# Half a chunk's second weight pass as pairs of 64-row matmuls, and a first normalisation shared by two engines

## What is computed

```python
xn = layernorm(x)                         # no scale, no shift, eps 1e-5
a  = silu(xn @ wA_gate.T)                 # 2048 x 2752
a[the half of each row that is smallest in |a|] = 0
s  = (a * (xn @ wA_up.T)) @ wA_down.T     # 2048 x 1024
g  = silu((silu(xn @ wB_gate.T) * (xn @ wB_up.T)) @ wB_down.T)
out = x + s * g
```

## Time and profile before

| what | us |
|---|---|
| median of three runs | 2845.15 |
| lowest and highest run | 2844.10, 2845.57 |
| the profiled execution, device time | 2844.23 |
| the same, span of the trace | 2842.5 |

### The profile page before, as it was taken

The page is one execution under the profiler, slowest core; times in us unless marked ns, Lnnn a source line. Parts: engine busy times, 40 slices in busy tenths (PEclk is TensorE's granted clock), DMA queues, the critical chain, the costliest instruction groups (busy, mean ns, idle before and its releaser), DMA issues.

```text
span 2842.5 us, 31407 instructions
## 1 busy us (share of the span) xinstructions
PE 2822.9 (99%) x12544; PEld 2349.2 (83%) x12544; DVE 1882.1 (66%) x2486; ACT 1209.3 (43%) x1202; POOL 661.6 (23%) x282
## 2 busy tenths in 40 slices
PE   7999999999999999999999999999999999999999
PEld 6888888888888888888888888888888888888887
DVE  3135989989312598998731168999872217899971
ACT  3335988223222477721122257771112225776110
POOL 5665443024644100000054410000005440000001
PEclk9999999999999999999999999999999999999999
DMA  6767888578432455556532245555653225555564
GB/s 223 244 237 279 291 288 287 200 258 321 161 97 98 160 194 194 194 195 240 200 133 96 94 175 193 194 194 192 245 185 132 96 92 189 192 192 193 192 226 173
DMA packets 100032, 549.95 MB, mean 193 GB/s; under 512 B 10992, under 2 KB 10992, under 8 KB 53104
## 3 DMA queue, kind: packets, MB, share of 16 engines
q1 hardware_dynamic: 99952, 548.97, 54.7%
HBM read 449.31 MB, written 99.61 MB: 193 GB/s over the span
## 4 chain that ended last, share of the span: by engine, by line
PE 99%; DVE 0%; POOL 0%; DMA 0%; issue 0%; DVEq 0%; SPq 0%; POOLq 0%
PE ps L383 33%; PE ps L481 11%; PE ps L482 11%; PE ps L483 11%; PE ps L456 11%; PE ps L459 11%; PE ps L457 11%; POOL hid_buf L729 0%; PE ps L438 0%; DVE stats L749 0%; DMA prods<-x 0%; POOL w_split L702 0%; DVE hid_buf L1027 0%; DVE prods L782 0%; DVE hid_buf L1025 0%
## 5 line engine op out<-in xcount | busy, mean ns | idle before, releaser
L702 POOL TENSOR_TENSOR w_split<-w_raw,w_split 128x1024 fp32r<-128x1024 f32 (+1 forms) x242 | 578.2, 2392 | 1700.1 <-ACT w_split L529 1522.3
L383 PE MATMUL ps<-w_split,hid_ring 128*128 128x512 f32 x4160 | 943.6, 389 | 0.0
L383 PEld LDWEIGHTS ps<-w_split,hid_ring 128*128 128x128 f32 x4160 | 781.0, 188 | 162.0
L815 DVE TENSOR_SCALAR_CACHE_REDUCE ranks<-key_buf,cand 128x2752 int16<-128x2752 f32 x248 | 763.0, 3076 | 5.8
L549 ACT ACTIVATE signs_row<-key_buf,cand 128x2752 bf16<-128x2752 f32 x248 | 642.4, 2590 | 191.0 <-DVE cand L824 181.3
L456 PE MATMUL ps<-w_split,xnT 128*128 128x512 f32 (+1 forms) x1408 | 541.4, 384 | 0.4 <-POOL w_split L702 0.4
L848 DVE TENSOR_TENSOR prods<-ps,key_buf 128x512 f32<-128x512 f32 (+1 forms) x96 | 61.1, 636 | 725.2 <-ACT key_buf L567 725.2
L457 PE MATMUL ps<-w_split,xnT 128*128 128x512 f32 (+1 forms) x1408 | 540.8, 384 | 0.0
L483 PE MATMUL ps<-xnT,w_split 128*128 128x512 f32 x1376 | 535.3, 389 | 0.0
L482 PE MATMUL ps<-xnT,w_split 128*128 128x512 f32 x1376 | 535.3, 389 | 0.0
L481 PE MATMUL ps<-xnT,w_split 128*128 128x512 f32 x1376 | 535.3, 389 | 0.0
(11 more groups left out here) (75 smaller groups left out, 1320.0 us busy)
## 6 DMA issues: line engine op xcount, KB each, us to landing
w_split<-split SPq DMA_DIRECT2D x280, 1024.0 KB, 4.8
w_raw<-w_a SPq DMA_DIRECT2D x160, 512.0 KB, 3.4
split<-w_split SPq DMA_DIRECT2D x64, 1024.0 KB, 6.4
split<-w_stage SPq DMA_DIRECT2D x22, 1024.0 KB, 6.3
w_raw<-w_b SPq DMA_DIRECT2D x42, 512.0 KB, 4.5
w_stage_raw<-wd_b SPq DMA_DIRECT2D x22, 512.0 KB, 4.6
w_raw<-wd_a SPq DMA_DIRECT2D x22, 512.0 KB, 4.7
prods<-x SPq DMA_DIRECT2D x16, 512.0 KB, 5.8
```

Of the source, the lines that this page charges most:

```text
L383: ins = pe.matmul(ps[:, 2 * t + half, :], h, w[:, half * TB:(half + 1) * TB], start=(first and n == 0), stop=(last and n == 1))
L702: pool.tensor_tensor(w_lo[q][:, 0:w], w_raw[q][:, 0:w], w_hi[q][:, 0:w].bitcast(F32), ALU.subtract).then_inc(lo_ready, 1)
L815: dve.tensor_scalar(ranks[:, :], keys[:, t, :], cand_f[:, t:t + 1], 0.0, ALU.is_lt, ALU.add, accum_out=counts[:, t:t + 1]).then_inc(sel_st ...
```

## The change

**Down projections.** In the last chunk of each, `down_tile` makes one pass (high plane, weights' high part). The pass with the weights' low part becomes `down_rows`, ahead of it, for all four tiles: for each tile two matmuls of 64 rows. One uses rows 0 to 63 for the first 512 output columns, the other rows 64 to 127 for the second 512. The second needs the hidden values' high part on rows 64 to 127, and ScalarE writes it there, into the low plane (a new instruction of 64x512 in `hid_split`). In `down_last` the waits for all three chunks and `down_rows` stand ahead of the loop over tiles.

**Start.** ScalarE normalises tiles 0 and 1 (ACT_NORM = 2) in one instruction each, as x times `rstd` plus `shift`; VectorE makes `shift` and normalises tiles 2 and 3. TensorE issues 84 transposes of the identity into the last bank (WARM) ahead of the real ones, and takes the real ones by tile, in the order 2, 3, 0, 1, for the first four banks and then for the other four. VectorE, no longer POOL, makes the low part of weight tile 0; ScalarE's high part of tile 2 moves behind its eight copies.

```diff
--- before.py
+++ after.py
@@ -72,6 +72,9 @@
 OUT_POOL = 3
 
 
+ACT_NORM = 2
+WARM = 84
+
 K_ORDER = (4, 5, 6, 7, 0, 1, 2, 3)
 
 STATS_AT = 6
@@ -201,6 +204,7 @@
         var = small("var", [NT])
         rstd = small("rstd", [NT])
         newton = small("newton", [NT])
+        shift = small("shift", [NT])
         found = small("found", [NT], U32)
         bit = small("bit", [NT], U32)
         cand = small("cand", [NT], U32)
@@ -230,6 +234,8 @@
         xres_landed = [sem(f"xres_landed{t}") for t in range(NT)]
         ln_step = sem("ln_step")
         xn_normed = sem("xn_normed")
+        xn_shift = sem("xn_shift")
+        xn_scaled = sem("xn_scaled")
         xn_turned = sem("xn_turned")
         xn_squares = sem("xn_squares")
         xn_hi = sem("xn_hi")
@@ -377,12 +383,20 @@
                     hi = hid_ring[:, s, 0, t * P:(t + 1) * P]
                     lo = hid_ring[:, s, 1, t * P:(t + 1) * P]
 
-                    passes = ((hi, w_hi[q]), (hi, w_lo[q])) if last else ((hi, w_hi[q]), (hi, w_lo[q]), (lo, w_hi[q]))
+                    passes = ((hi, w_hi[q]),) if last else ((hi, w_hi[q]), (hi, w_lo[q]), (lo, w_hi[q]))
                     for n, (h, w) in enumerate(passes):
                         for half in halves:
                             ins = pe.matmul(ps[:, 2 * t + half, :], h, w[:, half * TB:(half + 1) * TB],
-                                            start=(first and n == 0), stop=(last and n == 1))
+                                            start=(first and n == 0), stop=last)
                     return ins
+
+                def down_rows(q, s):
+
+                    for t in range(NT):
+                        for half in range(2):
+                            part = slice(half * TAIL, (half + 1) * TAIL)
+                            pe.matmul(ps[:, 2 * t + half, :], hid_ring[part, s, half, t * P:(t + 1) * P],
+                                      w_lo[q][part, half * TB:(half + 1) * TB], start=False, stop=False)
 
                 def down(m, hid_n, q, s, i=0, first=False, order=range(NT), bank_free=None):
                     weights(m, i)
@@ -395,11 +409,12 @@
 
                 def down_last(at, hid_n, mm, turn):
 
+                    for j in range(NJ - LAST, NJ):
+                        weights(at + j)
+                        pe.wait_ge(hid_lo, hid_n + j + 1)
+                    down_rows((at + NJ - 1) % RING, (NJ - 1 + turn) % RING)
                     for t in range(NT - 1):
                         for j in range(NJ - LAST, NJ):
-                            if t == 0:
-                                weights(at + j)
-                                pe.wait_ge(hid_lo, hid_n + j + 1)
                             ins = down_tile(t, (at + j) % RING, (j + turn) % RING, last=(j == NJ - 1))
                         ins.then_inc(mm, 1)
                     for half in range(2):
@@ -426,17 +441,28 @@
                         down(at + (NJ - 2), b * (2 * NJ) + hid_at + (NJ - 2), at % RING, turn)
                         weights(at + (NJ - 1))
                         pe.wait_ge(hid_lo, b * (2 * NJ) + hid_at + NJ)
+                        down_rows((at + 1) % RING, (turn + 1) % RING)
                         for t in range(NT):
                             ins = down_tile(t, (at + 1) % RING, (turn + 1) % RING, last=True)
                             ins.then_inc(mm if t < NT - 1 else tiles_done, 1)
 
                 if b == 0:
-                    for n, k in enumerate(K_ORDER):
-                        if n % (KC // 2) == 0:
-                            pe.wait_ge(xn_normed, NT if n == 0 else 2 * NT)
-                        for t in range(NT):
-                            ins = pe.transpose(ps[:, n, t * P:(t + 1) * P], prods[:, t, k * P:(k + 1) * P], ident[:, :])
-                        ins.then_inc(xn_turned, 1)
+                    for n in range(WARM):
+
+                        pe.transpose(ps[:, KC - 1, n % NT * P:(n % NT + 1) * P], ident[:, :], ident[:, :])
+
+                    tiles = (2, 3, 0, 1)
+                    for half in range(2):
+                        for t in tiles:
+                            if t >= ACT_NORM:
+                                pe.wait_ge(xn_normed, half * (NT - ACT_NORM) + (t - ACT_NORM + 1))
+                            elif half == 0:
+                                pe.wait_ge(xn_scaled, t + 1)
+                            for n in range(half * (KC // 2), (half + 1) * (KC // 2)):
+                                k = K_ORDER[n]
+                                ins = pe.transpose(ps[:, n, t * P:(t + 1) * P], prods[:, t, k * P:(k + 1) * P], ident[:, :])
+                                if t == tiles[-1]:
+                                    ins.then_inc(xn_turned, 1)
 
                 def a_products(n, q, gate, up, first_of_slab):
 
@@ -538,6 +564,9 @@
 
             def run(b, first_block):
                 def hid_split(dst, src, rows=P):
+                    if rows == TAIL:
+
+                        act.activation(hid_ring[TAIL:P, dst, 1, :], src[0:TAIL], ACT.Copy)
                     act.activation(hid_ring[0:rows, dst, 0, :], src[0:rows], ACT.Copy).then_inc(hid_hi, 1)
 
                 def count(n):
@@ -550,11 +579,16 @@
                                        accum_out=counts[:, t:t + 1]).then_inc(act_counted, 1)
 
                 if first_block:
-                    for m in range(AHEAD):
+                    for m in range(AHEAD - 1):
                         hi(b, m)
+                    act.wait_ge(xn_shift, 1)
+                    for t in range(ACT_NORM):
+                        act.activation(prods[:, t, 0:H], prods[:, t, 0:H], ACT.Identity, bias=shift[:, t:t + 1],
+                                       scale=rstd[:, t:t + 1]).then_inc(xn_scaled, 1)
                     for n, k in enumerate(K_ORDER):
                         act.wait_ge(xn_turned, n + 1)
                         act.activation(xnT[:, k, 0, :], ps[:, n, :], ACT.Copy).then_inc(xn_hi, 1)
+                    hi(b, AHEAD - 1)
                 if not first_block:
                     hi(b, AHEAD - 1)
 
@@ -712,8 +746,9 @@
                 for m in range(TILES):
                     if b == 0 and m == 0:
 
-                        pool.wait_ge(xn_normed, 2 * NT)
-                    elif b == 0 and m == AD0:
+                        pool.wait_ge(lo_ready, 1)
+                        continue
+                    if b == 0 and m == AD0:
 
                         pool.wait_ge(masked, NT)
                     if b == 0 and stage_at(m) is not None:
@@ -775,10 +810,16 @@
                 ins.then_inc(ln_step, 1)
                 assert done[0] + 1 == NORM_STEPS
 
-            def norm_apply(n):
+            def norm_shift():
+
+                dve.wait_ge(ln_step, NORM_STEPS)
+                dve.scalar_tensor_tensor(out=shift[:, :], in0=rstd[:, :], scalar=-1.0, in1=mean_var[:, :, 0],
+                                         op0=ALU.mult, op1=ALU.mult).then_inc(xn_shift, 1)
+
+            def norm_apply(n, tiles=range(NT)):
                 dve.wait_ge(ln_step, n * NORM_STEPS + NORM_STEPS)
                 for half in (slice(H // 2, H), slice(0, H // 2)):
-                    for t in range(NT):
+                    for t in tiles:
                         dve.tensor_scalar(prods[:, t, half], prods[:, t, half], mean_var[:, t, 0:1], rstd[:, t:t + 1],
                                           ALU.subtract, ALU.mult).then_inc(xn_normed, 1)
 
@@ -988,7 +1029,7 @@
                                 norm_rstd(b + 1)
                         elif j == NORM_AT:
                             norm_apply(b + 1)
-                            dve.wait_ge(xn_normed, (b + 2) * (2 * NT))
+                            dve.wait_ge(xn_normed, 2 * (NT - ACT_NORM) + (b + 1) * (2 * NT))
                         for square in x_squares[max(0, j - X_SQUARES_AT) * X_SQUARES_STEP:max(0, j - X_SQUARES_AT + 1) * X_SQUARES_STEP]:
                             ins = turn_x_squares(*square)
                             if square == x_squares[-1]:
@@ -1009,7 +1050,11 @@
             for t in range(NT):
                 norm_stats(0, t)
             norm_rstd(0)
-            norm_apply(0)
+            norm_shift()
+            norm_apply(0, range(ACT_NORM, NT))
+
+            dve.wait_ge(hi_ready, 1)
+            dve.tensor_tensor(w_lo[0], w_raw[0][:, :], w_hi[0].bitcast(F32), ALU.subtract).then_inc(lo_ready, 1)
             for b in range(NB):
                 run(b, b == NB - 1)
```

## The result

The changed kernel takes 2840.57 us (median of 20 runs) against 2844.53 (20 runs): 3.96 us less, ratio 0.9987 with a 95% interval of 0.9981 to 0.9993. The forecast was 2838.3, or 6.5 us less. The measured time lies within the range and on the forecast's side of no change, but the gain is 0.14%, so the likeliest case, over 0.2%, did not come. It also lies just outside the 2835.5 to 2840.5 that the forecast gave to its own case; only the widening of the range for other cases took it in.

A forecast was written before the change was run, and what follows sets the result against it. TensorE bounds the kernel, busy 2822.9 of 2842.5 us. Start -3.2, BD -3.63, AD of blocks 1 and 2 -1.41, tail -0.45, switches +14c: -6.5 at c = 0.16, forecast 2838.3, range 2835.2 to 2843.8.

The forecast's parts named there:

- the likeliest case: Whole kernel: the forecast's own case, gain over 0.2%, spanning 2835.5 to 2840.5 us; chance 0.60, with 0.15 of it short of 0.2%.
- Pairs side by side: Down projections' last chunk: 8 half-row matmuls take 4 slots, saving 0.907 us in each of 8 projections, 7.25 in all.
- That rival's price: Down projections: the two matmuls of a pair run in turn, saving no slots; 2842.5 to 2845.2 us, chance 0.22.
- The switch, c = 0.16: Every down projection: each of two changes between 128 and 64 rows costs 0.16 us, the pipe's drain alone; 14c in the sum.
- the upper end of 0.29: Cost of one row-size switch: 0.16 us draining, 0.10 slow restart and 0.03 for the load; the total would be 2840.1.
- All else must merely stay hidden: Whole kernel: time is saved only by fewer matmul slots, earlier first matmul, shorter tail or less of TensorE's one 0.4 us wait.
- 0.13 spare: End of BD: first tile's silu ends 605.89, next phase wants the bank 606.02; four BDs save 3.63 - 8c.
- the stall grows to 1.5, saves 0: AD of block 0, next phase A: tile 2 still comes at 736.16 because of POOL, so 0.63 us lost becomes 1.5.
- AD of blocks 1 and 2, 0.2 late: Next phase A's first matmul about 0.06 us late for VectorE, then slow restart: 0.2 together; both ADs save 1.41 - 4c.
- Tail: AD of block 3: VectorE product, POOL add and VectorE's add hang on the third tile's last matmul; saves 0.45 - 2c.
- The start, 3.2: Kernel start: first 512-column matmul at 17.4 us instead of 20.58, 3.2 saved, bounds 2.2 to 3.5.
- The clock rival: Start: warm-up never speeds up, 84 transposes at 0.214 take 18.0 us; +4.9, 2849.7 us, chance 0.04.

The follow-up runs named there:

- pairs by tile: Changed kernel with each tile's 64-row pair directly ahead of its full pass, except in the last AD: 2847.14 us, 6.6 more than the changed kernel.
- ScalarE's new order: Changed kernel plus POOL's extra wait, with ScalarE's split of AD's hidden chunk 2 ahead of the silus, chunk 3 ahead of weight tile 2's high part: 2838.69 us.
- the kernels with the first tile early: Changed kernel with projections' last two chunks tile by tile, not last AD: 2842.07 us; plus POOL's extra wait 2841.27; that in blocks 1 to 3 only 2838.79.
- POOL's wait: Changed kernel with one more POOL wait, so the fourth tile's low part in block 0's phase B starts behind the search's first round: 2839.57 us, ratio 0.9983.

## Why the prediction was right, and where it was not

- **Pairs side by side: right.** 64-row matmuls cost half a slot each; in turn they would have cost 7.1 us more, by the run on the same rows. That rival's price, 0.91 a projection, was right too.
- **The switch, c = 0.16: too small.** It is 0.23 in the changed kernel and 0.20 with pairs by tile, between the value taken and the upper end of 0.29. The step that failed is "the drain alone, because loads are issued ahead elsewhere". The first matmul behind a switch is 0.09 or 0.10 late, less than the 0.16 of the drain, but the second is another 0.11 late. That is the slow restart, which the forecast had in its upper end and left out of c. The loads behind a switch begin with their matmuls, not ahead of them. Seven hundredths in 14 switches are 1.0 us, and by the forecast's own working any c above 0.21 takes the gain below 0.2%. The Trainium skill (TensorEngine Tiling, Key Properties) has the array drain at a change of mode; rows with 0.20 to 0.23 us a switch agree. The same skill (TensorE: Matmul & The Clock Gate, Part 3) lets the matmuls of different row groups start about 4 ns apart; here the two of a pair start 3 to 10 ns apart, most of them 3 or 4, which agrees.
- **"All else must merely stay hidden": not true of phase B.** The forecast had the change of A and B of block 0 at zero and never asked what else there keeps its own pace. The search does, it gates POOL's weight parts, and the new start put a POOL instruction 0.02 us in front of a short copy: +0.8, proved by one wait that moved POOL away. The Trainium skill (SBUF, Who interferes with whom) has VectorE and POOL share a port pair under an exclusive lock that the first to start holds to its end. That the copy ends when POOL does, at 263.2, agrees; no page tells that the two would meet here.
- **BD, "0.13 spare": the wrong reader.** The bank was nearly in time. But behind the four silus ScalarE has chunks 2 and 3 of the next projection, and behind those VectorE works at 6.4 us a chunk against 5.44. As seen from TensorE this chain started 1.35 us later (1.17 instead of 2.52 before AD), and 0.95 us of waits followed. Undone by ScalarE's new order.
- **AD of block 0, "the stall grows to 1.5, saves 0": wrong place, and 0.3 short.** AD and the next phase A took 0.3 longer together than before. The wait for tile 2 shrank to 0.1, because POOL's three additions and tile 2's low part took 7.58 and 2.85 us instead of 8.05 and 3.37. So it is in every profile with the pairs of all tiles ahead of the full passes and block 0's chunks in order, with or without waits in AD. It is not so with the new start alone (8.04 and 3.37), nor with pairs by tile (8.0 and 3.37), where the first product comes earlier. That POOL meets less of VectorE when the products come later is argued, not shown. BD, AD and A together save 0.14, not 0.59; 0.14 of the difference is c.
- **AD of blocks 1 and 2, 0.2 late: 0.34** (0.19 ahead of phase A and 0.15 in it), and 0.06 more between BD and AD. The mechanism was right; the kernels with the first tile early start phase A of these blocks without a gap.
- **Tail: right in its chain.** 0.3 saved over block 3 instead of 0.72 is c again, 0.28 in both projections, and the same 0.06; the last 0.1 stays open. The chain runs over product, addition and VectorE's stretched last addition (1.89 us).
- **The start, 3.2: 2.7** in this profile and 3.1 in the one taken again. ScalarE's normalisation was costed by silu (1.03 for one) and takes 1.24 and 1.23, 2.38 for both together; the rest is when x lands (VectorE normalises from 12.89 here, from 12.51 before and in the profile taken again). That the warm-up ran 1.1 us shorter than forecast, with 14 slow transposes instead of 24, was luck without effect. The clock rival did not come: 84 transposes took 10.9 us, where at 0.214 they would take 18. The granted clock reads 1.00 in the slow and in the fast stretch, so it does not tell them apart. The rule of the Trainium skill (TensorE: Matmul & The Clock Gate, Part 4), that the full clock does not engage for transposes, does not fit this: the pace doubled while only transposes ran.

Of the 3.2 us by which the profiles fell short of the forecast, c makes 1.0, phase B 0.8, the start 0.5, block 0's AD 0.3 net, and the phase boundaries and the tail 0.6.

## What to carry to other kernels

When one engine is 99% busy and an edit moves its schedule by a few microseconds, list every chain that keeps a pace of its own (here a search and VectorE's transposes) and ask how much lead it has; the gain ends where the smallest lead does. Shortening the last step of a phase also moves its first result towards the end, so follow each reader of that result and all that is queued behind it, not only the buffer it frees. Row pairs pay if several run between two switches: four pairs save 0.91 and two switches take 0.46.

## What the hardware showed that was not expected

- A 128x4 predicated copy on VectorE takes 2.38 us instead of 0.16 when a POOL subtraction of 128x1024 has begun 0.02 us before. All five profiles read with the new start, the warm-up and no extra wait have it. In the first one with POOL's wait and the one without warm-up POOL begins 0.4 us behind the copy's start, as it did in the kernel before, and the copy takes 0.16.
- The time until the pace of transposes doubles varies from execution to execution: 84 of them took 10.75 to 12.35 us with the same code. By their start times the pace goes from 0.213 to 0.109 us each, 2.8 us after the first one at the soonest and 6.2 at the latest. The granted clock read 1.00 throughout.
- A change of row size is paid twice: the first matmul behind it starts 0.09 or 0.10 us late, and the second follows it after 0.33 or 0.34 us instead of 0.227. The first lasts 0.49 to 0.50 us, the others 0.39. The second half of this also follows a plain stall, as at 736.20 before.
- Two matmuls of 64 rows on different rows and banks start 3 to 10 ns apart. On the same rows they take turns at the pace of full ones.
